# Scan stage of a four-stage block: the product dBu of four of the sixteen states moves from VectorE to GpSimd

## The reference

```python
def _L1_attn_ref(x, W_in, conv_w, conv_b, W_x, W_dt, b_dt, A_log, D, W_out):   # x: (2, 2048, 128), INTER = 256
    raw, gate = jnp.split(x @ W_in, 2, axis=-1)
    h = jax.nn.silu(conv(raw, conv_w) + conv_b)                   # causal, 4 taps
    ts, Bmat, C = jnp.split(h @ W_x, [64, 80], axis=-1)           # B and C: 16 values per position
    dt = jax.nn.softplus(ts @ W_dt + b_dt)
    dA = jnp.exp(dt[..., None] * -jnp.exp(A_log))                 # (.., 256 channels, 16 states)
    dBu = dt[..., None] * Bmat[:, :, None, :] * h[..., None]
    # state = dA * state + dBu along the positions;  y = sum over the 16 states of state * C
    y = (scan(dA, dBu, C) + h * D) * jax.nn.silu(gate)
    return y @ W_out
```

## Time and profile before

| what | value |
|---|---|
| median of 3 runs | 1652.56 us (1647.0 to 1653.2) |
| the profiled execution's own time | 1651.93 us |
| its span | 1649.9 us |
| scan stage in the span | about 624 to 1204 us |
| busy over the span: TensorE, VectorE, ScalarE, GpSimd | 1215.8, 994.2, 769.9, 715.3 us |
| VectorE scans (line 1221) | 256 of 1267 ns |

### The profile page before, as it was taken

One profiled execution on the slowest core, in us unless ns is written; L12 is line 12 of the kernel. 1 busy time (PEld: TensorE's weight loads), 2 busy tenths in 40 slices (PEclk: granted clock), 3 DMA queues, 4 the chain that ended last, 5 costly groups with the idle time before them and its releaser, 6 DMA issues. The chain is left out here.

```text
span 1649.9 us, 18990 instructions
## 1 busy us (share of the span) xinstructions
PE 1215.8 (74%) x5585; PEld 586.1 (36%) x5585; DVE 994.2 (60%) x1432; ACT 769.9 (47%) x1266; POOL 715.3 (43%) x601
## 2 busy tenths in 40 slices
PE   3544489797897976777978778885768288888883
PEld 1111234242332432332333323332225266666663
DVE  4765645445464316989888797989921833444344
ACT  3553433425344345756657475655524233333334
POOL 0121221312222005767677676857631444444533
PEclk8676789899999977999989898998975599999996
DMA  5000000000000000000000000000001011111114
GB/s 180 0 0 0 0 1 0 1 1 0 0 0 0 0 26 13 13 13 14 25 1 26 13 13 0 0 0 1 1 0 45 12 30 35 34 35 34 33 29 156
DMA packets 13401, 32.37 MB, mean 20 GB/s; under 512 B 3344, under 2 KB 3536, under 8 KB 13104
## 3 DMA queue, kind: packets, MB, share of 16 engines
q1 hardware_dynamic: 8784, 22.10, 4.0%
q0 software_dynamic: 4544, 9.32, 1.9%
HBM read 22.56 MB, written 8.85 MB: 19 GB/s over the span
## 5 line engine op out<-in xcount | busy, mean ns | idle before, releaser
L1158 POOL TENSOR_TENSOR prod<-hs,csb 128x1024 f32<-128x1024 f32 x128 | 303.6, 2372 | 150.7 <-DVE hs L1221 149.1
L1221 DVE TENSOR_TENSOR_SCAN hs<-dA,carry,pD 128x512 f32<-128x512 f32 x256 | 313.8, 1267 | 17.6 <-issue 12.4
L970 PE MATMUL pY<-prod,const 128*128 128x512 f32 x512 | 251.8, 615 | 15.1 <-DVE h L1206 11.2
L1081 ACT ACTIVATE dA<-dt,negA 128x512 f32<-128x512 f32 x256 | 170.2, 718 | 2.6 <-POOL dt L1130 2.5
L1086 ACT ACTIVATE csb<-pC 128x512 f32<-128x512 f32 x128 | 76.2, 595 | 177.6 <-PE pC L984 177.5
L970 PEld LDWEIGHTS pY<-prod,const 128*128 128x128 f32 x512 | 98.9, 197 | 133.8 <-issue 112.5
L1844 DVE CAST x<-pX 128x256 f16<-128x256 f32 x71 | 30.2, 425 | 174.1 <-issue 129.7
L1414 PE MATMUL pR<-x,moe_hi 128*128 128x128 f16 x568 | 130.4, 230 | 4.1 <-issue 2.0
L1672 POOL DMA_INDIRECT moe_outs<-y,to x71 | 71.1, 1002 | 134.5 <-ACT y L1600 130.7
L1415 PE MATMUL pR<-x,moe_hi 128*128 128x128 f16 x568 | 125.9, 222 | 0.0
L1416 PE MATMUL pR<-x,moe_lo 128*128 128x128 f16 x568 | 125.8, 221 | 0.0
(11 more groups left out here) (339 smaller groups left out, 2870.3 us busy)
## 6 DMA issues: line engine op xcount, KB each, us to landing
raw<-moe_w SPq DMA_DIRECT2D x12, 512.0 KB, 3.5
room<-moe_outs SPq DMA_DIRECT2D x8, 512.0 KB, 8.5
X<-xT SPq DMA_DIRECT2D x4, 512.0 KB, 4.5
hidw<-hid_w SPq DMA_DIRECT2D x1, 2048.0 KB, 9.9
moe_rows<-xt SPq DMA_DIRECT2D x8, 256.0 KB, 2.0
outT<-X SPq DMA_DIRECT2D x8, 256.0 KB, 2.0
g<-moe_rows,source POOLq DMA_INDIRECT x71, 2.5
moe_outs<-y,to POOLq DMA_INDIRECT x71
```

The source lines that it names most:

```text
L970: last = nc.tensor.matmul(YB[c][:], G.ident, prod[:, slot(b, n), c, :], start=n == 0, stop=n == DST - 1)
L1081: last = nc.scalar.activation(dA[:, slot(b, n), c, :], dt[:, b, c, :], ACT.Exp, scale=negA[:, c, n:n + 1])
L1158: nc.gpsimd.tensor_tensor(prod[:, slot(b, n), :, :], hs[:, slot(b, n), :, :], csb[:, slot(b, n), :, :].to_broadcast([P, CB, N]), ALU.mult)\
L1221: last = nc.vector.tensor_tensor_scan(hs[:, slot(b, n), c, :], dA[:, slot(b, n), c, :], dBu(n, c), carry[:, b, n, c:c + 1], ALU.mult, ALU.add)
```

## The change

HELPED names four states, 4, 7, 9 and 11; OWN the other twelve. For a state in HELPED:

- three states earlier (LEAD = 3) TensorE spreads its B into the bank of C, `CC`, after C of that state has been copied out; ScalarE copies it to SBUF (`bsb`); GpSimd multiplies it with dtu into one of two SBUF buffers (`helped`) after its product of that state;
- TensorE's matmul for it at its own place, and VectorE's product, are gone;
- dA of that state is written by ScalarE into the two PSUM banks of `DD` that would have held dBu: chunk 1 once the scan of two states ago is done, chunk 0 once the first scan of the state before is done (`scan0`);
- VectorE scans chunk 1 first, then chunk 0, with dA from PSUM and dBu from SBUF.

Before C of the following state TensorE waits until the copy of B has been read out (`b_in`). To make room in SBUF, `raw` and `scaled` lose their second buffer, so each piece of the next stage's weights is loaded only when GpSimd has finished the one before.

```diff
+    HELPED = (4, 7, 9, 11)
+    OWN = tuple(n for n in range(DST) if n not in HELPED)
+    LEAD = 3
-        scaled = sb("scaled3", [P, B, N])
+        scaled = sb("scaled3", [P, N])
+        bsb = sb("bsb3", [P, 1, N])
+        helped = sb("helped3", [P, 2, CB, N])
-        raw = sb("raw3", [P, 2, 2 * FFN])
+        raw = sb("raw3", [P, 2 * FFN])
+        def among(t, b, n, members):
+            return t * (B * len(members)) + (b * len(members) + sum(m <= n for m in members))
+        def before_helped(n):
+            i = HELPED.index(n)
+            return HELPED[i - 2] + 1 if i >= 2 else HELPED[i - 2] + 1 - DST
...
@@ SyncE
-                if i >= 2:
-                    sp.wait_ge(S["w_low"], i - 1)
+                if i >= 1:
+                    sp.wait_ge(S["w_low"], i)
...
@@ TensorE, body
-                    wait_past(pe, S["scan"], state(t, b, n) - 2)
-                    nc.tensor.matmul(bcastB(n), G.sel[:, n, :], split[:, b, :], start=True, stop=True)\
-                      .then_inc(S["bcastB"], 1)
+                    if n in OWN:
+                        wait_past(pe, S["scan"], state(t, b, n) - 2)
+                        nc.tensor.matmul(bcastB(n), G.sel[:, n, :], split[:, b, :], start=True, stop=True)\
+                          .then_inc(S["bcastB"], 1)
                     wait_past(pe, S["c_in"], state(t, b, n) - 1)
+                    if n - 1 + LEAD in HELPED:
+                        pe.wait_ge(S["b_in"], among(t, b, n - 1 + LEAD, HELPED))
                     nc.tensor.matmul(CC[:], G.sel[:, DST + n, :], split[:, b, :],
                                      start=True, stop=True).then_inc(S["bcastC"], 1)
...
+                    if n + LEAD in HELPED:
+                        pe.wait_ge(S["c_in"], state(t, b, n))
+                        nc.tensor.matmul(CC[:], G.sel[:, n + LEAD, :], split[:, b, :], start=True, stop=True)\
+                          .then_inc(S["bcastH"], 1)
                     if n >= LAG:
                         accumulate(t, b, n - LAG)
...
@@ ScalarE, body
+                    if n in OWN:
...
+                    else:
+                        act.wait_ge(S["scan"], state(t, b, n) - 2)
+                        nc.scalar.activation(dBu(n, 1), dt[:, b, 1, :], ACT.Exp, scale=negA[:, 1, n:n + 1])
+                        act.wait_ge(S["scan0"], among(t, b, n, HELPED))
+                        nc.scalar.activation(dBu(n, 0), dt[:, b, 0, :], ACT.Exp, scale=negA[:, 0, n:n + 1])\
+                          .then_inc(S["dA"], 1)
...
+                    if n + LEAD in HELPED:
+                        act.wait_ge(S["bcastH"], among(t, b, n + LEAD, HELPED))
+                        wait_past(act, S["dBuH"], among(t, b, n + LEAD, HELPED) - 1)
+                        nc.scalar.activation(bsb[:, 0, :], CC[:], ACT.Copy).then_inc(S["b_in"], 1)
...
@@ GpSimd, body
                     keep(t, b, n)
+                    if n + LEAD in HELPED:
+                        k = among(t, b, n + LEAD, HELPED)
+                        pool.wait_ge(S["b_in"], k)
+                        wait_past(pool, S["scan"], state(t, b, 0) - 1 + before_helped(n + LEAD))
+                        nc.gpsimd.tensor_tensor(helped[:, HELPED.index(n + LEAD) % 2, :, :], dtu[:, b, :, :],
+                                                bsb[:, :, :].to_broadcast([P, CB, N]), ALU.mult)\
+                          .then_inc(S["dBuH"], 1)
...
@@ VectorE, scan
                     for c in range(CB):
                         last = nc.vector.tensor_tensor_scan(hs[:, slot(b, n), c, :], dA[:, slot(b, n), c, :],
                                                             dBu(n, c), carry[:, b, n, c:c + 1],
                                                             ALU.mult, ALU.add)
+                        if c == 0 and n + 1 in HELPED:
+                            last.then_inc(S["scan0"], 1)
+                else:
+                    dve.wait_ge(S["dBuH"], among(t, b, n, HELPED))
+                    for c in (1, 0):
+                        last = nc.vector.tensor_tensor_scan(hs[:, slot(b, n), c, :], dBu(n, c),
+                                                            helped[:, HELPED.index(n) % 2, c, :],
+                                                            carry[:, b, n, c:c + 1], ALU.mult, ALU.add)
```

More of the change, by code:

```diff
@@ L868, in phase_ssm @@
                  "h xproj ts_in split1 rest1 split2 split3 split4 dt_in magnitude expm log1p relu "
-                 "dt dtu bcastB bcastC dA c_in dBu scan kept prod acc y ygated "
-                 "down squaredC varianceC logC rstdC scaledC addedC w_in0 w_in1 w_high w_scaled w_low").split()
+                 "dt dtu bcastB bcastC bcastH b_in dBuH scan0 dA c_in dBu scan kept prod acc y ygated "
+                 "down squaredC varianceC logC rstdC scaledC addedC w_in w_high w_scaled w_low").split()
         S = mem.enter_context(semaphores_of_phase(nc, "ssm_", names))
@@ L908, in _ @@
             for i in range(PIECES):
-                if i >= 2:
-                    sp.wait_ge(S["w_low"], i - 1)
-                sp.dma_start(raw[:, i % 2, :], G.moe_w13[:, i, :] if i < E else w2[:, i - E, :])\
-                  .then_inc(S[f"w_in{i % 2}"], 16)
+                if i >= 1:
+                    sp.wait_ge(S["w_low"], i)
+                sp.dma_start(raw[:, :], G.moe_w13[:, i, :] if i < E else w2[:, i - E, :])\
+                  .then_inc(S["w_in"], 16)
         @block.tensor
@@ L1054, in prep @@
                         act.wait_ge(S["dt_in"], chunk(t, b, c))
-                        wait_past(act, S["dBu"], state(t, b, 0) - 1 - DST)
+                        wait_past(act, S["dBu"], among(t, b, -1, OWN) - len(OWN))
+                        wait_past(act, S["dBuH"], among(t, b, -1, HELPED) - len(HELPED))
                         nc.scalar.activation(dtu[:, b, c, :], Q[c][:], ACT.Abs, bias=col("b_dt", c))\
@@ L1078, in body @@
                         act.wait_ge(S["dt"], at(t, b))
-                    wait_past(act, S["scan"], slot_before(t, b, n))
-                    for c in range(CB):
-                        last = nc.scalar.activation(dA[:, slot(b, n), c, :], dt[:, b, c, :], ACT.Exp,
-                                                    scale=negA[:, c, n:n + 1])
-                    last.then_inc(S["dA"], 1)
+                    if n in OWN:
+                        wait_past(act, S["scan"], slot_before(t, b, n))
+                        for c in range(CB):
+                            last = nc.scalar.activation(dA[:, slot(b, n), c, :], dt[:, b, c, :], ACT.Exp,
+                                                        scale=negA[:, c, n:n + 1])
+                        last.then_inc(S["dA"], 1)
+                    else:
[4 more added lines that the diff above has]
+                          .then_inc(S["dA"], 1)
                     act.wait_ge(S["bcastC"], state(t, b, n))
@@ L1229, in body @@
                         dve.wait_ge(S["dtu"], at(t, b))
-                    dve.wait_ge(S["bcastB"], state(t, b, n))
-                    wait_past(dve, S["scan"], state(t, b, n) - 1)
-                    if n % 2:
+                    if n in HELPED:
+                        pass
+                    elif n % 2:
+                        dve.wait_ge(S["bcastB"], among(t, b, n, OWN))
+                        wait_past(dve, S["scan"], state(t, b, n) - 1)
                         nc.vector.tensor_tensor(dBu(n, 0), dtu[:, b, 0, :], bcastB(n), ALU.mult)
-                        last = nc.vector.tensor_tensor(dBu(n, 1), dtu[:, b, 1, :], bcastB(n), ALU.mult)
+                        nc.vector.tensor_tensor(dBu(n, 1), dtu[:, b, 1, :], bcastB(n), ALU.mult).then_inc(S["dBu"], 1)
                     else:
-                        last = nc.vector.tensor_tensor(DD[:, 0:CB, :], dtu[:, b, :, :],
-                                                       bcastB(n).unsqueeze(1).to_broadcast([P, CB, N]), ALU.mult)
-                    last.then_inc(S["dBu"], 1)
+                        dve.wait_ge(S["bcastB"], among(t, b, n, OWN))
+                        wait_past(dve, S["scan"], state(t, b, n) - 1)
+                        nc.vector.tensor_tensor(DD[:, 0:CB, :], dtu[:, b, :, :],
+                                                bcastB(n).unsqueeze(1).to_broadcast([P, CB, N]), ALU.mult)\
+                          .then_inc(S["dBu"], 1)
                     scan(t, b, n)
```

27 lines of the change are left out of this document (14 added, 13 removed).

## The result

The changed kernel takes 1671.07 us in the median of four runs (1671.06 to 1673.09), the kernel before 1651.19 in the median of four (1647.0 to 1653.2). The ratio is 1.0123 with a 95% interval of 1.0107 to 1.0138: slower by 20 us, and 7 us above the upper end of the range. The profiled execution is one of these runs, 1671.09 us.

The account below looks back on a forecast made before the run. It took no engine alone as the bound: VectorE, TensorE, GpSimd and ScalarE were close, with waits around states 4 to 7. 1651.9 + 1.8 (seven tiles) - 4.8 (last tile) = 1648.9, so 1649 us; range 1632 to 1664.

Parts of the forecast that it names:

- 62.9 of 72, not the bound: GpSimd per tile: four more multiplications, 9.5 us on 53.4, make it busy 62.9 of 72 us without being the bound.
- State 7: State 7: TensorE's C broadcast waits for ScalarE's copy of B for state 9; dBu 8 comes 0.9 us later.
- rival C: State 7's C broadcast held behind the copy of B, clock low in all seven tiles: +13 us, 1665; chance 0.15.
- the clock: TensorE's x projection: slow tiles rise from three to four of seven; a slow one costs 1.65 us more.
- States 8 to 12: VectorE saves dBu 9 and 11, 2.64 us, but dBu 10 comes 1 us later; a fast tile gains 0.5 us.
- rival B: dBu 9 and 11 come through in all tiles, without state 7's hold: 23 us faster, 1629; chance 0.20.
- State 4, worth 0: State 4: dBu 5 still waits for TensorE's broadcast, so the removed dBu 4 turns into idle time: 0 us.
- The last tile: Last tile, no convolution in TensorE's queue: 0.85 us plus three removed dBu of 1.32 each, 4.8 us gained.
- The costs without a row: Scan with dA in PSUM and dBu in SBUF: 0; ScalarE's dA write to PSUM: 0.718 us, 3.4 us either way.
- rival D: GpSimd late with dtu by 4 us at the start of six tiles: +19 us, 1672; chance 0.05.
- The single buffers: Weight buffer freed near 872.4, transfer lands 3.5 us after issue, ScalarE wants it at 880.8: hidden.
- forecast +1.8: Seven tiles that prepare a next one: 272.7 us after against 270.9 before, from y to dBu 12, 1.8 lost.

Follow-up runs that it names:

- e3: e2 plus four products per tile on GpSimd that nothing reads, VectorE still making all its dBu: 1684.26 us, ratio 1.0191.
- e6: The changed kernel with ScalarE's copy of B for state 9 moved before the Silu block in state 6: 1663.52 us, ratio 1.0067.
- e9: e1 plus four unused products of dtu and dt per tile on GpSimd, without the path of B: 1659.7 us, ratio 1.0057.
- e2: e1 plus the path of B (TensorE's broadcast into CC, ScalarE's copy, the wait before the next C), no GpSimd product: 1670.23 us, ratio 1.0107.
- e4: The changed kernel with the halo copy on GpSimd and the cast to mid replaced by a subtraction from PSUM: 1664.59 us, ratio 1.0073.
- e10: e3 with the halo copy on GpSimd and the cast to mid replaced by a subtraction from PSUM: 1673.62 us, ratio 1.0136.
- e7: The changed kernel with the edits of both e4 and e6: 1660.92 us, ratio 1.0052.
- e1: The kernel before with single buffers for the weight pieces and scaled, nothing else changed: 1650.76 us, ratio 0.9993.
- e5: e2 with ScalarE's copy of B for state 9 moved before the table loads and Silu in state 6: 1658.82 us, ratio 1.0037.
- e8: The changed kernel with states 13 and 15 helped instead of 4, 7, 9, 11, LEAD 12, halo copy on GpSimd: 1628.41 us, ratio 0.9847.
- e11: e8 with the halo copy back on VectorE: 1632.78 us, ratio 0.989.

## Why the prediction was wrong

**The copies on VectorE: the step that was missing.** The prediction put no cost of GpSimd's new work on VectorE into its sum. "62.9 of 72, not the bound" was right about GpSimd and wrong as a cost of nothing. The order of time after shows each small copy of VectorE beside a running product of GpSimd:

```profile
...
863.34 2.34 POOL L1199 TENSOR_TENSOR helped<-dtu,bsb 128x1024 f32<-128x1024 f32 x1
...
864.62 1.09 DVE L1227 COPY xn<-xn 128x3 f32<-128x3 f32 x1
...
```

```profile
...
902.45 2.35 POOL L1199 TENSOR_TENSOR helped<-dtu,bsb 128x1024 f32<-128x1024 f32 x1
...
902.92 2.16 DVE L1237 CAST mid<-sq 96x512 bf16<-96x512 f32 x1
...
905.01 1.22 DVE L1288 TENSOR_TENSOR pD<-dtu,pD 128x1024 f32<-128x1024 f32 x1
...
907.03 2.36 POOL L1191 TENSOR_TENSOR prod<-hs,csb 128x1024 f32<-128x1024 f32 x1
...
908.81 0.73 DVE L1240 COPY split<-mid 32x512 bf16<-32x512 bf16 x1
...
```

The product that began at 863.34 ends at 865.68, the halo copy at 865.71. The product of 902.45 ends at 904.80 and the cast at 905.08; that of 907.03 ends at 909.39 and the split copy at 909.54. So the copy is reported as started, stands until GpSimd's instruction is done, and ends a short time after it. That time is the same in all thirteen traces: of the copies that began beside a running GpSimd instruction, the 30 halo copies ended 22 to 30 ns after it and the 64 casts 278 to 287 ns after it, however long they had stood; the held split copies of e3, e6, e9 and the changed kernel ended 143 to 150 ns after it. Copies that began with none running took 141 to 146, 396 to 425 and 281 to 285 ns. In the kernel before, GpSimd stood waiting for the scan at each halo copy, and six of the seven casts took 744 to 751 ns, held by the end of a weight split; the prediction didn't look at these three. The Trainium skill, "SBUF — State Buffer", section "SBUF: two separate sides", states this: a VectorE operation in a two-port mode, or with two SBUF inputs against a GpSimd operation that reads SBUF, and a GpSimd operation exclude each other for a whole instruction, whichever starts first. The trace agrees: copies from SBUF to SBUF wait, while instructions of VectorE with an operand in PSUM don't. In the changed kernel, dBu takes 1226 ns beside a running GpSimd instruction and 1230 without one, and the scan with dA in PSUM 1267 and 1270. The prediction had no case for this. Its price is e9, 8.5 us without any other part of the change, and 14 with the path of B in place (e3 over e2). Moving the halo copy takes 7.0 to 7.2 us of it away in state 2 (e4, e10).

**State 7: the right mechanism, mis-sized.** "Its next C broadcast (state 7) waits until that copy has read the shared PSUM bank" is what happens, and rival C named it. The tile at the full level lost 1.1 us in states 6-7 (10.5 against 9.4; 0.9 forecast), a slow one 1.7 us more (12.2; 1.65 forecast). Off was **the clock**: "I count four slow ones". Six of seven were slow in the trace after and six in e2. For states 6-7 the forecast's terms make 7 x 0.9 + 4 x 1.65 - 3 x 0.5 = 11.4 us, measured 16.2. The other traces point the same way. With 2.9 to 3.2 us of idle time before it (changed kernel, e2, e3, e4, e10) the projection was slow in 32 of 35 tiles, with 2.09 us (e6, e7) in 5 of 14, and with 1.88 us (before, e1, e5, e8, e9, e11) in 9 of 42. The prediction raised the idle time by 2 us and the count by only one tile. Which tiles fall no run settles. Rival C had all seven tiles slow and nothing won back, and gave 1665. Its first condition held but for one tile, its second didn't (states 8-11 won 4.0), and the time is 6 us above its own, since it had no held copies either.

**States 8 to 12.** Forecast was dBu 12 half a microsecond earlier in a fast tile, which is 1.4 us won a tile in these states, 10 in seven. Measured: 115.6 to 111.5, 4.0. From e2 to e3, with GpSimd's products added, these states lose 4.7 (115.6 to 120.2), and from e3 to the changed kernel they gain 8.7. That the holding of cast and split copy is what the products cost there is shown by e9 and e10; that the changed kernel would be 4.7 us shorter without it is not, since VectorE has to wait for B of state 10 in any case (1.90 us in e4). dBu 10 came 33.5 us after y (905.01 - 871.49) against 30.6, so rival B is out. That the two products would not bring their full 18.5 us was right, and e7 shows why: dBu 10 hangs on TensorE.

**State 4, worth 0:** right. VectorE goes from y to the scan of state 4 at once and then idles 5.58 us before dBu 5 in the tile shown; 5.4 was forecast.

**The last tile:** 3.1 us gained, 4.8 forecast. Without removed work the kernels have 71.2 to 73.4, with it 68.1 to 68.7, so it is the removed work.

**The costs without a row:** the scan was 1268 ns (1267 to 1271 bounded it). ScalarE's write of dA to PSUM took 692 and 688 ns against 714 to SBUF, inside the bounds; over 64 instructions that is 1.5 us of busy time. The Trainium skill, "ScalarE: Activation LUTs", section "Step-by-step: what each stage is for", calls writing PSUM the faster side, and the trace agrees. The reordered waits, 0.07 us for each of the twelve states with their own dBu, were in no term of the sum. **GpSimd, rival D:** VectorE's waits in the stage after have one for dtu, 10.5 us before the first tile, as before. Out. **The single buffers:** nothing (e1).

Summed over seven tiles, forecast +1.8 and measured +22.6: the size of states 6-7 explains 4.8 of the difference, state 2 6.3, states 8-11 6.0, the turn of the loop 2.7. What is left has both signs: -2.9 in states 0-1, +2.3 in 3-5, +2.0 in the rest of 12 on. In whole-kernel time the experiments give 0 for the buffers, 18 for the path of B and 14 for the products; what was removed gives 13 back, and this last number is only the remainder to the measured 1671.

## What to carry to other kernels

Before work is moved to GpSimd because it has time, list VectorE's instructions that go from SBUF to SBUF and lie beside it: each can be held until the GpSimd instruction beside it ends (here up to 1.9 us), however small it is. A shared bank couples engines: an added user that stands behind a long block (here two table loads and a Silu) holds back everything that the bank's next writer has queued, and it belongs ahead of the block or in another stretch; ahead of the block it cost 6 us here instead of 18. Take work off an engine only where it is the late one: two states at the tile's end brought 24 us, four around its waits lost 20. (Part of that difference is B's copy away from the Silu block, the halo copy on GpSimd and two products fewer; 20 us of the 24 are in the states where the products were removed.) Keep the order of waits when code is moved, or measure it by itself.

## What the hardware showed that was not expected

- A copy of 3 columns took 143 ns on VectorE with GpSimd idle and 1100 with GpSimd at work; a cast of 512 columns 2191 instead of 698. The ends of these copies stand at a fixed distance behind the end of GpSimd's instruction.
- Moving a halo of 3 x 128 values to GpSimd and turning a cast into a subtraction from PSUM are worth 6.5 and 10.6 us in two kernels; by the table it is the halo alone (7.0 and 7.2 us in state 2), and the subtraction costs in state 8 what it saves in 9 and 10.
- TensorE's level after a longer idle time: the same four passes took 1.93 us in one tile and 2.50 to 3.52 in the six others. When they are spared, the low level can come two states later (e7).
- Four kernels have 2.7 us of idle VectorE at the loop's turn, with four or five instruction-fetch packets just before it.
- The gap between dBu and its scan is 36 ns in every kernel with the old order of waits and 105 in every kernel with the new one.
- What follows on the stage varies by some microseconds from run to run: e2's profiled run had its stage end 16 us later than the kernel before but took 7 us more (1658.99 against 1651.93), and e11's ended 13 us after e8's but took 7.7 more. So the parts of the stage are compared in the table, and the kernels by their medians.
